# The gated layer of a graph-and-expert network: one product moved from the node stage into the edge stage, and a narrower last row block

## The reference, cut to what matters

```python
Wh = x @ W_w + W_b;  Uh = x @ U_w + U_b;  Vh = x @ V_w + V_b      # x: layer norm of the rows
sigma = sigmoid((Wh * attn_l)[src] + (Wh * attn_r)[dst])          # one row of 256 for each edge
sum_sigma_h = segment_sum(Vh[src] * sigma, dst)
sum_sigma   = segment_sum(sigma, dst)
h = Uh + sum_sigma_h / (sum_sigma + 1e-6)
x = x + relu(layernorm(h) * gamma + beta)
```

## Time and profile before

| | |
|---|---|
| median of three runs | 3003.66 us (3002.97 to 3009.3) |
| the profiled execution's own time | 3003.86 us |
| its span, first to last instruction | 3002.2 us |
| busy: PE, DVE, ACT, POOL | 83%, 78%, 39%, 45% of the span |
| granted TensorE clock, mean | 0.908 |
| `stage_gated_in` | about 1638 to 1737 us |
| `stage_strips` | about 1738 to 2818 us; the next stage begins at 2830 |
| last stage (second experts) | to the end of the span |

### The profile page before, as it was taken

The page is one execution under the profiler, slowest core; times in us unless marked ns, Lnnn a source line. Parts: engine busy times, 40 slices in busy tenths (PEclk is TensorE's granted clock), DMA queues, the critical chain, the costliest instruction groups (busy, mean ns, idle before and its releaser), DMA issues. The chain is left out here.

```text
span 3002.2 us, 50772 instructions
## 1 busy us (share of the span) xinstructions
PE 2495.9 (83%) x17111; PEld 1245.4 (41%) x17164; DVE 2350.3 (78%) x5375; ACT 1158.3 (39%) x2327; POOL 1364.5 (45%) x1627
## 2 busy tenths in 40 slices
PE   5999979999969999966997947677676777767598
PEld 3666655333355333344665512233332333323365
DVE  6888889999959999977444847777777777777477
ACT  5777720000020000012222435666666666566421
POOL 2999920000000000001830867777777777775055
PEclk8999989999989999976998977888888888888799
DMA  4000000000020000031432687888888888888343
GB/s 125 12 11 12 10 36 15 15 15 15 5 82 15 15 15 15 5 100 45 121 96 64 203 249 238 250 259 256 259 255 252 257 257 260 255 252 250 121 150 107
DMA packets 210756, 373.53 MB, mean 124 GB/s; under 512 B 52554, under 2 KB 140559, under 8 KB 208682
## 3 DMA queue, kind: packets, MB, share of 16 engines
q0 software_dynamic: 75536, 238.14, 26.4%
q1 hardware_dynamic: 131737, 128.66, 13.5%
q10 hardware_dynamic: 3200, 3.21, 0.4%
HBM read 324.84 MB, written 50.04 MB: 125 GB/s over the span
## 5 line engine op out<-in xcount | busy, mean ns | idle before, releaser
L1167 PE MATMUL dense_p_o<-dense_W,feat 128*32 128x512 f32 x7200 | 789.8, 595 | 17.5 <-DVE dense_W L1099 17.5
L1099 DVE SCALAR_TENSOR_TENSOR dense_W<-layer_B,steep,cnt 128x512 f32<-128x512 f32 x1200 | 796.7, 750 | 3.3 <-DVE dense_W L1099 2.0
L2466 POOL DMA_INDIRECT Wd<-tab_d,ixq x544 | 519.4, 955 | 171.1 <-issue 166.2
L1167 PEld LDWEIGHTS dense_p_o<-dense_W,feat 128*32 128x32 f32 x7200 | 281.9, 110 | 494.5 <-issue 390.3
L1577 POOL MEMSET edst<- 128x782 int32 x1 | 0.8, 750 | 921.9 <-POOLq L1216 921.9
L2644 PE MATMUL strips_p_sg<-strips_sv,strips_oh 128*32 128x512 f32 x2000 | 313.6, 704 | 101.0 <-DVE strips_sv L2509 101.0
L2632 PE MATMUL strips_p_b<-strips_wrs,strips_ohT 96*128 96x256 bf16 x1000 | 177.8, 308 | 208.8 <-DVE strips_ohT L2480 190.6
L732 POOL TENSOR_SCALAR mix_L<-mix_back,encode_lowT 128x128 bf16<-128x128 f32 x520 | 328.6, 650 | 18.7 <-PE mix_p_c L891 18.6
L2573 ACT ACTIVATE strips_p_s<-strips_tv 128x1024 f32<-128x1024 f32 (+1 forms) x250 | 225.2, 901 | 157.3 <-DVE strips_sv L2509 144.5
L1123 ACT COPY dense_part<-dense_p_o 128x512 f32<-128x512 f32 x36 | 18.8, 596 | 639.7 <-PE dense_p_o L1167 639.7
L2466 POOL DMA_INDIRECT strips_G<-tab_d,ixq x240 | 228.9, 954 | 73.1 <-issue 72.8
(11 more groups left out here) (543 smaller groups left out, 3899.3 us busy)
## 6 DMA issues: line engine op xcount, KB each, us to landing
strips_row<-dlr_d SPq DMA_DIRECT2D x250, 96.0 KB
ew<-in_ew SPq DMA_DIRECT2D x16, 1024.0 KB, 5.4
layer_B<-rise_d SPq DMA_DIRECT2D x12, 1024.0 KB, 4.6
hx_d<-hrow SPq DMA_DIRECT2D x24, 512.0 KB, 2.7
Wd<-tab_d,ixq POOLq DMA_INDIRECT x544
Wd<-in_fWd SPq DMA_DIRECT2D x8, 1024.0 KB, 9.2
tab_d<-feat SPq DMA_DIRECT2D x50, 130.0 KB, 1.9
tab_d<-gated_in_rowg SPq DMA_DIRECT2D x25, 256.0 KB, 2.0
```

Source lines behind the costliest of these rows:

```text
L1099: o = nc.vector.scalar_tensor_tensor(out=out, in0=rise, scalar=C.steep[:, q * H + h:q * H + h + 1], in1=count, op0=ALU.max, op1=ALU.mult)
L1167: m = nc.tensor.matmul(p_o[c % 2][h * MT:(h + 1) * MT, a, 0:n], feat[:, q, h, lo:lo + MT], W[t % 3][:, h, 0:n], start=(q == 0), stop=(q == ...
L2466: gp.indirect_dma_start(out=G[n % RING][:, j, :], out_offset=None, in_=C.tab3[:, :], in_offset=bass.IndirectOffsetOnAxis(ap=index, axis=0) ...
```

## The change

In `stage_gated_in` the product U is no longer made. W and V stand side by side in one PSUM bank and are made by one 512-column matmul for each half of the depth, with two bias matmuls. The transposed block (`xT_d`) is stored in place of U. The buffers are deeper (four for transposed blocks, rows and products, five for the parts). The split is shared out otherwise: DVE makes the f32 product only, ACT casts the first part (`first_part`) and the second (`second_part`), POOL keeps the two subtractions (`rest`, `third_part`), which are two pieces of its loop now.

In `stage_strips` SP loads the transposed block (`xTu`) in place of U, and PE makes U by `project(b)` in the first step of the next block, into the last 256 columns of `p_h`; DVE adds it from there. SP loads the next transposed block behind `project`, between two index rows. The normalised block `xn` has one buffer. The last block's eight whole steps are two strips wide on all engines (`wide`, `shown`), but the masks and sums of its first step stay four wide.

The second way makes U in `stage_gate`; that code is skipped here.

```diff
@@ stage_gated_in, gpsimd
-                    if b >= late:
-                        split(b - late)
+                def rest(b):
+                    k = b % NW
+                    gp.wait_ge(s_w0, b + 1)
+                    nc.gpsimd.tensor_tensor(wf[k][:, :], wf[k][:, :], wp[k][:, 0, :], ALU.subtract).then_inc(s_sub, 1)
+                def third_part(b):
+                    k = b % NW
+                    gp.wait_ge(s_w1, b + 1)
+                    nc.gpsimd.tensor_tensor(wp[k][:, 2, :], wf[k][:, :], wp[k][:, 1, :], ALU.subtract).then_inc(s_sp, 1)
...
+                for b in range(NB + late + 1):
                     if b < NB:
                         gather(b)
+                    if late <= b < NB + late:
+                        rest(b - late)
+                    if b >= late + 1:
+                        third_part(b - late - 1)
@@ stage_gated_in, vector
-                    nc.vector.tensor_tensor(wp[m][:, 0, :], p_a[k][:, 0, 0:D], ar[:, :], ALU.mult).then_inc(s_row, 1)
@@ stage_gated_in, scalar
+                def first_part(b):
+                    act.wait_ge(s_row, b * 2 + 2)
+                    if b >= NW:
+                        act.wait_ge(s_wd[b % NW], 16 * (b // NW))
+                    nc.scalar.copy(wp[b % NW][:, 0, :], wf[b % NW][:, :]).then_inc(s_w0, 1)
+                def second_part(b):
+                    act.wait_ge(s_sub, b + 1)
+                    nc.scalar.copy(wp[b % NW][:, 1, :], wf[b % NW][:, :]).then_inc(s_w1, 1)
...
-                    if b >= 1:
-                        taken(b - 1, (b - 1) % 2)
+                    if 2 <= b <= NB + 1:
+                        taken(b - 2, (b - 2) % 4)
+                    if 2 <= b <= NB + 1:
+                        first_part(b - 2)
+                    if b >= 4:
+                        second_part(b - 4)
@@ stage_gated_in, tensor
-                    for a, lo, w in ((0, 0, D), (1, D, 2 * D)):
-                        for kc in range(KC):
-                            nc.tensor.matmul(p_a[k][:, a, 0:w], xT[k][:, kc * P:kc * P + P], w3[:, kc, lo:lo + w], start=(kc == 0), stop=False)
-                        nc.tensor.matmul(p_a[k][:, a, 0:w], onesS[:, :], C.b3S[:, lo:lo + w], start=False, stop=True).then_inc(s_a, 1)
+                    to = p_a[b % 4][:, :, :].rearrange("p a d -> p (a d)")
+                    for kc in range(KC):
+                        nc.tensor.matmul(to, xT[b % 4][:, kc * P:kc * P + P], w3[:, kc, :], start=(kc == 0), stop=False)
+                    nc.tensor.matmul(p_a[b % 4][:, 0, :], onesS[:, :], C.b3S[:, 0:D], start=False, stop=False)
+                    nc.tensor.matmul(p_a[b % 4][:, 1, :], onesS[:, :], C.b3S[:, 2 * D:3 * D], start=False, stop=True).then_inc(s_a, 1)
@@ stage_strips
         def wide(g):
-            return H if g % QC < QR else 1
+            return strips(g) if g % QC < QR else 1
+        def shown(g):
+            return H if g % QC == 0 or g % QC >= QR else strips(g)
...
                     def load_u(b):
-                        sp.dma_start(U[b % 2][:, :], C.u_d[b * P:(b + 1) * P, :]).then_inc(s_u[b % 2], 16)
+                        if b >= 1:
+                            sp.wait_ge(s_up, b)
+                        sp.dma_start(xTu[:, :], C.xT_d[b * P:(b + 1) * P, :]).then_inc(s_u, 16)
...
-                        if i == 0 and b >= 1 and b + 1 < NB:
-                            sp.wait_ge(s_ur, b)
+                        if i == 8 and 0 <= b and b + 1 < NB:
                             load_u(b + 1)
...
-                            nc.vector.tensor_tensor(h, h, U[b % 2][:, :], ALU.add).then_inc(s_ur, 1)
+                            nc.vector.tensor_tensor(h, h, p_h[:, F - D:F], ALU.add).then_inc(s_ur, 1)
@@ stage_strips, tensor
+                    def project(b):
+                        if b == 0:
+                            pe.wait_ge(s_wu, 16)
+                            pe.wait_ge(s_ones, 1)
+                        else:
+                            pe.wait_ge(s_ur, b)
+                        if b >= 2:
+                            pe.wait_ge(s_he, FC * (b - 1))
+                        pe.wait_ge(s_u, 16 * (b + 1))
+                        for kc in range(KC):
+                            nc.tensor.matmul(p_h[:, F - D:F], xTu[:, kc * P:kc * P + P], wu[:, kc, :], start=(kc == 0), stop=False)
+                        nc.tensor.matmul(p_h[:, F - D:F], ones[:, :], C.b3S[:, D:2 * D], start=False, stop=True).then_inc(s_up, 1)
...
                     def group(g):
                         if g + 2 < NG4:
                             expand(g + 2)
+                        if g % QC == 0 and g > 0:
+                            project(g // QC - 1)
...
                     def tail(b, i):
+                        if i == 0 and b == NB - 1:
+                            project(b)
...
+                            if i == QC + 7 and b < NB - 1:
+                                pe.wait_ge(s_ur, b + 2)
...
+                            pe.wait_ge(s_ur, min(b + 3, NB))
```

More of the change, by code:

```diff
@@ L2147, in _ @@
-                for k in range(3):
-                    sp.wait_ge(s_wd[k], 16 * ((NB + 2 - k) // 3))
+                        turned(b)
+                    if 1 <= b <= NB:
+                        back(b - 1, (b - 1) % 4)
+                    if b >= 4:
+                        parts(b - 4)
+                for k in range(NW):
+                    sp.wait_ge(s_wd[k], 16 * ((NB + NW - 1 - k) // NW))
+                for k in range(4):
+                    sp.wait_ge(s_xTd[k], 16 * ((NB + 3 - k) // 4))
@@ L2149, in _ @@
                 sp.wait_ge(s_dw, 32)
[L2150 to L2151 removed]
+                for k in range(4):
+                    sp.wait_ge(s_rowd[k], 16 * ((NB + 3 - k) // 4))
             @block.gpsimd
             def _(gp):
[L2155 to L2161, removed]
+                def rest(b):
+                    k = b % NW
+                    gp.wait_ge(s_w0, b + 1)
+                    nc.gpsimd.tensor_tensor(wf[k][:, :], wf[k][:, :], wp[k][:, 0, :], ALU.subtract).then_inc(s_sub, 1)
@@ L2263, in _ @@
                 normal(0, 0)
-                for b in range(NB + 1):
+                for b in range(NB + 4):
                     if b + 2 < NB:
@@ L2642, in sums @@
                             pe.wait_ge(s_tot, 2 * b - 2)
-                        for j in range(H):
+                        for j in range(shown(g)):
                             t = nc.tensor.matmul(p_sg[b % 2][j * QP:(j + 1) * QP, :], oh[g % 4][:, j, :], sv[g % 2][:, j % wide(g), :],
@@ L3042, in _ @@
                 with when_even(C, act, 0):
+                    for b in range(NB):
+                        act.wait_ge(s_up, b + 1)
+                        if b >= 2:
+                            act.wait_ge(s_us[b % 2], 16 * (b // 2))
+                        nc.scalar.copy(U[2 + b % 2][:, :], (p_l, p_r)[b % 2][:, 0:D]).then_inc(s_uc, 1)
                     def root(c):
@@ L3080, in _ @@
                 with when_even(C, pe, 0):
+                    pe.wait_ge(s_wu, 16)
+                    pe.wait_ge(s_ones, 1)
+                    for b in range(NB):
+                        pe.wait_ge(s_ux[b % 2], 16 * (b // 2 + 1))
+                        if b >= 2:
+                            pe.wait_ge(s_uc, b - 1)
+                        to = (p_l, p_r)[b % 2][:, 0:D]
+                        for kc in range(KC):
+                            nc.tensor.matmul(to, U[b % 2][:, kc * P:kc * P + P], wu[:, kc, :], start=(kc == 0), stop=False)
+                        nc.tensor.matmul(to, ones[:, :], C.b3S[:, D:2 * D], start=False, stop=True).then_inc(s_up, 1)
+                    pe.wait_ge(s_uc, NB)
                     pe.wait_ge(s_wd, 64)
```

150 lines of the change are left out of this document (83 added, 67 removed).

## The result

The changed kernel takes 3013.36 us (median of 20 runs, 3004.6 to 3018.55). The kernel before, run beside it 20 times, takes 3009.09 us (3000.77 to 3010.43), not the 3003.66 of the three runs from which the forecast started. The ratio is 1.0019, with a 95% interval of 1.0012 to 1.0026: 5.7 us slower (3.6 to 7.8; the two medians alone are 4.3 us apart). The forecast of 3004 us lay 0.3 us above its starting point; of the 9.4 us by which it missed the time, 5.4 are that starting point and the rest is in the sum.

A forecast was written before the change was run, and what follows sets the result against it. The node stage was to become bound by the gather loop, while POOL's gathers keep pacing the edge stage. 3003.86 + 8.3 (node) - 8.4 (last block) + 0.5 (tail) = 3004.3, so 3004 us; range 2998 to 3010, with rivals 2991 to 3018.

The forecast's parts named there:

- The gather loop: Node stage: a gather is issued only after the add two blocks before; 3.70 us a block against 3.24, +8.3 us.
- The turn: Node stage: from DVE's add through ACT, POOL and the gather's landing back to DVE, 7.4 us for two blocks.
- The begin and the drain of the node stage: Block 0's cold product (0 to +1 us) and the drain behind the last add, the same 13.5 us (0 to +3).
- The edge stage's steady part: Edge stage up to the last block: `project` hidden in PE's pause, POOL's pace stays; 0 us (-5 to +12).
- The last block: Edge stage's last block: narrower steps bring the last add at 2779.5 instead of 2787.91, -8.4 us (-10 to -5).
- The tail: Behind the last step: PE makes U of block 24 ahead of block 22's logits, +0.5 us (0 to +1.5).
- the cold PE: Rival, node stage: PE at half clock costs up to 4.2 us a block, 17.3 us in all, 3013; chance 0.18.
- the narrow steps that save nothing: Rival, last block: waits for pieces of blocks 21 to 23 fill the freed time, 3013 us; chance 0.07.
- The unbound loop: Rival, node stage: the gather loop doesn't bind, 2.9 us a block, -6 in place of +8.3, 2990; chance 0.10.

The follow-up runs named there:

- late5: Changed kernel with POOL's `rest` and `third_part` one iteration earlier in its loop (late = 5 in place of 6): 3075.9 us, ratio 1.0224 to the kernel before.
- u_alone: Changed kernel with the last row block's steps four strips wide again, so only U's move remains: 3017.8 us, ratio 1.0036 to the kernel before.
- both `project` kernels: Changed kernel with `project`'s two products and bias made two or three times over in each edge-stage block: 3012.3 us (1.0015) and 3014.1 us (1.0020).
- before_again: The kernel before, unchanged, profiled once more: 3006.4 us in one run.
- pad: The kernel before with an unused HBM buffer of xT_d's size added ahead of hx_d: 3003.1 us in one run.
- narrow_alone: The kernel before with only the last row block's regular steps made two strips wide: 3001.8 us, ratio 0.9975 to the kernel before.
- late8: Changed kernel with POOL's `rest` and `third_part` two iterations later (late = 8) and rings of seven buffers in place of five: 2996.3 us, ratio 0.9963.
- late7: Changed kernel with POOL's `rest` and `third_part` one iteration later (late = 7 in place of 6): 2996.2 us, ratio 0.9956 to the kernel before.

## Why the prediction was right, and where it was wrong

**The gather loop: right in mechanism, the term too small.** The turn was put at 7.4 us and +8.3 for 18 blocks; it measured 7.66 early in the stage and 7.92 later, 3.86 us a block, 18 x (3.86 - 3.24) = +11.2. The links, from the rows above: add to ACT's first copy 2.52 us for 2.15, since the add takes 0.85 in place of 0.48; a gather's issue and POOL's subtraction (L2167) run beside it, and the subtraction takes 0.84 for 0.68; the copies and `second_part` 1.23 for 1.16; POOL's piece and the gather's issue 0.90 for 0.9; the landing 3.01 for 3.2. In `late5`, where the adds are alone and take 0.48, the turn is 7.06 (1702.06 to 1709.12). The later growth is the landing: 3.42 us in the turn from 1706.76 to 1714.68. The prediction had costed each link as it runs alone, and missed that the add takes longer where POOL's pieces now run beside it; the last section says how far the traces show why.

**The begin and the drain of the node stage.** Left at nothing, with a possible loss; they gave back 3.7 us in this profile (first gather to block 6 19.36 us for 21.64, last add to the edge stage's first 28.74 for 30.20). The stage as a whole is +7.4 here, but 119.6 against 108.7 us in the means of four profiles each (changed, u_alone and both `project` kernels against before, before_again, pad and narrow_alone): +10.8. In these means the 18 blocks are +12.5 us and begin and drain together -1.6, so more than half of the 3.7 is spread between these two profiles.

**By the Trainium skill**, "DMA: Bandwidth & Descriptors", section "Anatomy of one DMA", the turn would have been 6.5 us and the stage unchanged. The gathers of these blocks land in 2.9 to 3.6 us, never in the estimated 2.3, and the stage grew: the measurement decides.

**The edge stage's steady part: right**, at 0 within the spread of the profiles (997.9 to 1003.5 us), and with more room than was claimed: with three copies of `project` PE is busy 778.2 us in the 24 blocks and 711.3 in the kernel before, 2.8 us more in each block, and they are hidden.

**The last block: right.** Forecast -8.4 and a last add 30 us after the first. Five of the eight profiles with narrow steps have 29.8 to 29.9; against the mean of the wide ones (38.4) the mean of all eight, 30.4, is -8.0. The changed kernel's own profile has 31.0, since PE runs near the low level of 1.2 GHz there in step 5 (granted 0.58 from 2779.8 to 2783.8), whose multiplication waits for ACT and so for PE's transposes. The other two longer ones, `late8` with 31.3 and `narrow_alone` with 31.7, have stretches of 4 us at 0.50 and 0.57 in this block as well; in the five the clock is 1.00 throughout. PE's rows, of the changed kernel and then of `late7`, which had 1.00 there after the same 2.04 us of idling; what made the difference isn't shown:

```profile
2780.02 1.58 PE L2677 MATMUL strips_p_sg<-strips_sv,strips_oh 128*32 128x512 f32 x4
2781.53 1.12 PE L2751 MATMUL strips_p_h<-ident,strips_HT 128*128 128x128 f32 x4
2782.44 0.63 PE L2716 MATMUL strips_p_h<-ident,strips_xn 128*128 128x128 f32 x2
```

```profile
2765.26 1.05 PE L2677 MATMUL strips_p_sg<-strips_sv,strips_oh 128*32 128x512 f32 x4
2766.25 0.66 PE L2751 MATMUL strips_p_h<-ident,strips_HT 128*128 128x128 f32 x4
2766.74 0.38 PE L2716 MATMUL strips_p_h<-ident,strips_xn 128*128 128x128 f32 x2
```

From the begin of the first to the end of the third that is 3.05 us against 1.86, a difference of 1.19 us and so all of it (31.04 against 29.84). **The tail** behind it, from the last add to the begin of ACT's last copy: 28.87 us for 29.08 in these two profiles, but 29.1 for 28.8 in the means of the six kernels with one `project` and the four without, so +0.3 for +0.5.

**The sum.** Measured terms, from the means: node +10.8, edge 0, last block -8.0, tail +0.3, together +3.1 us, and +5.5 if the 2.4 of the dense stage are the change's; the ratio says +5.7 (3.6 to 7.8). The forecast's sum was +0.4. The term that was mis-sized is the gather loop: +8.3 forecast, +11.2 in this profile and +12.5 in the means, of which the begin and the drain hide a part. The forecast's own range, 2998 to 3010, didn't hold the measured 3013.36, and more than half of the miss is the starting point; that the wide range of 2991 to 3018 held it is in part luck, since its upper end came from rivals that were not at work. **The rivals:** the cold PE named 3013, the time that came, and so did the narrow steps that save nothing; `narrow_alone` shows the second wrong. For the first the clock did fall to 0.90, and it came nearer than the mean of a block's products (50.38 / 18 = 2.8 us of PE, under the turn's 3.86) says. In the turn ahead of the one shown, PE made a product at the low clock and DVE waited for it:

```profile
1671.55 3.35 PE L2324 MATMUL gated_in_p_ag<-gated_in_w,gated_in_xTg 128*128 128x512 f32 x4
...
1675.15 0.42 DVE L2220 TENSOR_TENSOR gated_in_rowg<-gated_in_p_ag,gated_in_al 128x256 f32<-128x256 f32 x1 [1.91 <-PE gated_in_p_ag L2326]
```

The add of block 10 (1676.02) then follows without a wait for its gather. The same happens ahead of the adds of blocks 16, 20 and 24 (1.25 to 1.85 us of waiting for PE), and there the gather still lands 0.58 to 0.89 us later. So the way through a cold PE is nearly as long as the gather's, but doesn't lengthen the turn: it is 7.59 us for block 10, and 7.66 and 7.64 for blocks 12 and 13, where PE ran at full clock. The Trainium skill, "TensorE: Matmul & The Clock Gate", section "HAM oscillation", describes the loop of waits and lost clock: the trace agrees with the fall, not with its setting the time. The unbound loop was put at 2.9 us a block: that is what `late7` shows (2.86), once one iteration is added.

**A version that beats both:** `late7`, 0.9956 of the kernel before (13 us less, 9 to 17), and 17 us below the changed kernel by the medians, 19 by the ratios, for one digit.

## What to carry to other kernels

Where in-order engines pass a block around, count the distance in blocks from each wait to the work that feeds it; a piece cut from the bound engine and put last in another engine's turn can close a loop that is longer than any engine's work, and one iteration of lag or one place in the turn opens it again. Here PE's shorter busy time came with a falling granted clock, and the loop's waits were what the fall followed; look for such a loop first, and only then at the clock. Cost the links of such a loop as they run beside their new neighbours, not as they run alone.

## What was not expected

DVE's add took 0.66 to 0.91 us in seven of the 19 blocks 6 to 24, each time with POOL's subtraction beginning 0.3 to 0.6 us behind its start, right behind a gather's issue, and 0.47 to 0.48 otherwise; the subtraction was longer as well (0.84 for 0.68). The Trainium skill, "SBUF — State Buffer", section "SBUF: two separate sides", has DVE and GpSimd share one port pair, held by one instruction to its end while the other is blocked. That they hinder each other agrees. In `late7` one of the pair at a time is longer, as a lock of the first comer would have it; two pairs, of blocks 15 and 22:

```profile
1689.62 0.47 DVE L2196 SCALAR_TENSOR_TENSOR X<-gated_in_yb,kept,X 128x256 f32<-128x256 f32 x1
1689.67 0.95 POOL L2167 TENSOR_TENSOR gated_in_wf<-gated_in_wf,gated_in_wp 128x256 f32<-128x256 f32 x1
...
1709.48 0.68 POOL L2167 TENSOR_TENSOR gated_in_wf<-gated_in_wf,gated_in_wp 128x256 f32<-128x256 f32 x1
1709.69 0.77 DVE L2196 SCALAR_TENSOR_TENSOR X<-gated_in_yb,kept,X 128x256 f32<-128x256 f32 x1
```

Where the subtraction begins 0.05 to 0.12 us behind the add (blocks 11 to 18), the add takes its 0.47 to 0.48 and the subtraction 0.87 to 0.95; where the subtraction was already running (six blocks), it takes 0.68 to 0.69 and the add ends 0.29 to 0.30 us behind it. The changed kernel's seven pairs don't fit: both are longer, and in four of them the subtraction begins 0.49 us or more behind the add's start, when an add of 0.48 would have been over. What holds up the add there isn't shown.
